# A stack of four graph networks on one core: sets by group, the entry to the second network and the output by node tile, angles on 128 rows

## The reference

```python
x = x + L0(h, ...)   # 7 graph convolutions with softmax over edges and a virtual node; a layer norm at the end
x = x + L1(h, ...)   # 4 blocks: conditioned layer norm, attention over edges, conditioned layer norm, dense pair
x = x + L2(h, ...)   # x @ wc + mean over edges of (x @ wn)[dst] + bias
x = x + L3(h, edge_attr, path_coeffs, src, dst, path_indices)
```

```python
x1 = x_nodes[src].reshape(-1, 16, 32)
x2 = x_edges.reshape(-1, 16, 32)
contrib = path_coeffs[None, :, None] * x1[:, i1, :] * x2[:, i2, :]     # 64 paths (i1, i2, i3)
edge_out = zeros.at[:, i3, :].add(contrib)
out = zeros.at[dst].add(edge_out.reshape(-1, 512))
```

## Time and profile before

| | us |
|---|---|
| median of 3 runs | 857.91 (856.36 to 860.02) |
| the profiled execution, own time | 857.5 |
| its span, first to last instruction | 855.7 |
| busy PE / DVE / ACT / POOL | 775.5 / 611.4 / 217.7 / 129.7 |
| mean granted TensorE clock | 0.968 of full |
| last network, from its first plain product | 541.3 to 855.7 |

### The profile page before, as it was taken

How to read it: one execution, slowest core, us unless ns; L and a number is a source line. 1 busy time by engine, 2 the same in 40 slices (tenths; PEclk the granted TensorE clock), 3 DMA queues, 4 the chain that set the end, 5 groups by cost and what they waited for, 6 DMA issues and landing times.

```text
span 855.7 us, 10601 instructions
## 1 busy us (share of the span) xinstructions
PE 775.5 (91%) x2972; PEld 501.2 (59%) x2972; DVE 611.4 (71%) x1581; ACT 217.7 (25%) x456; POOL 129.7 (15%) x145
## 2 busy tenths in 40 slices
PE   6888898898898999999999999889889997997998
PEld 2556455365365766667567554565676673683673
DVE  8876675675676534553553553799999999999895
ACT  6633123123121311311312212203304304304300
POOL 6000000000101000000000002611531451340000
PEclk9899999999999999999999999899989997997999
DMA  5813323214131423433342100742523443330000
GB/s 198 306 58 103 111 84 124 108 53 159 61 124 69 142 87 130 149 115 117 117 147 75 62 1 31 256 132 77 183 86 99 126 120 98 108 89 1 0 1 25
DMA packets 39175, 88.38 MB, mean 103 GB/s; under 512 B 3890, under 2 KB 4159, under 8 KB 39135
## 3 DMA queue, kind: packets, MB, share of 16 engines
q1 hardware_dynamic: 34496, 72.71, 25.2%
q0 software_dynamic: 4640, 15.21, 6.0%
HBM read 86.86 MB, written 1.05 MB: 103 GB/s over the span
## 4 chain that ended last, share of the span: by engine, by line
PE 51%; DVE 24%; issue 15%; DVEq 7%; ACT 1%; POOL 1%; DMA 0%; ACTq 0%; SPq 0%; POOLq 0%
PE PS L753 40%; DVE big L1504 8%; PE PS L1043 6%; DVE tail L1495 4%; DVEq L1470 3%; DVE tail L1514 2%; DVE prods L1514 2%; DVEq L1474 2%; DVE h L1128 1%; PE PS L909 1%; PE PS L762 1%; DVEq L1504 1%; DVEq L1514 1%; PE PS L858 1%; PE PS L954 1%
## 5 line engine op out<-in xcount | busy, mean ns | idle before, releaser
L753 PE MATMUL PS<-big 128*128 128x512 f32 (+1 forms) x368 | 137.2, 524 | 1.7 <-DVE big L1398 1.7
L1495 DVE SCALAR_TENSOR_TENSOR tail<-big,coef 128x448 f32 (+3 forms) x216 | 130.7, 616 | 3.1 <-issue 3.1
L1504 DVE TENSOR_TENSOR big<-big,tail 128x448 f32 (+3 forms) x216 | 120.9, 560 | 4.1 <-DVE tail L1495 3.1
L753 PEld LDWEIGHTS PS<-big 128*128 128x128 f32 x368 | 67.4, 190 | 63.6 <-issue 54.8
L753 PE MATMUL PS<-hT,big 128*128 128x256 f32 (+1 forms) x512 | 87.0, 329 | 4.4 <-ACT hT L678 4.4
L576 POOL DMA_INDIRECT big<-h_rows,src_i x58 | 77.2, 1331 | 85.6 <-PE PS L1043 62.9
L753 PEld LDWEIGHTS PS<-hT,big 128*128 128x128 f32 x512 | 77.5, 191 | 15.2 <-ACT hT L678 7.3
L550 POOL TENSOR_TENSOR rstd<-var,minus_half 128x1 f32<-128x1 f32 x36 | 21.6, 601 | 421.3 <-DVE var L1102 419.2
L1043 PE MATMUL PS<-big,hotd_more 128*128 128x512 f32 x176 | 76.5, 592 | 0.0
L1057 PE MATMUL PS<-hotd_more,tail 128*128 128x256 f32 x256 | 59.5, 387 | 0.0
L1043 PEld LDWEIGHTS PS<-big,hotd_more 128*128 128x128 f32 x176 | 33.4, 190 | 41.6 <-issue 41.6
...
## 6 DMA issues: line engine op xcount, KB each, us to landing
...
```

The costliest lines, as they stand in the source:

```text
L753: return pe.matmul(o, lhsT, rhs, start=start, stop=stop)
L1495: dve.scalar_tensor_tensor(out=prod[:, slot, tiles, :], in0=xs[:, tiles, bass.ds(i1, EXT)], scalar=coef[:, row:row + 1], in1=xe[:, tiles, ...
L1504: dve.tensor_tensor(o, o, prod[:, slot, tiles, :], ALU.add)._wait_ge(path_step, max(product_at[slot], added_at[0])).then_inc(path_step, 1)
```

## The change

- `SETS_OF` goes from 8, 6, 5, 5, 5 to 8, 7, 6, 6, 4, with new orders of the blocks for groups 1 to 4. The turns of the sets' sums in the last group stand between four sets instead of five.
- VectorE fills nothing of the sums any more: ScalarE fills tiles 0 to 6, GpSimd the rest, and VectorE waits for two parts instead of three. VectorE fills the PSUM half of set 3 with zeros, between the copies of picked rows, and set 3 starts on it without a start flag.
- The entry to L1: `first_norm` does all steps of node tile 0 and then all of node tile 1; GpSimd's roots follow that order; TensorE makes the first tables once the last convolution's statistics are there, and 3 fill products follow them instead of 6.
- L2: ScalarE takes each turned tile out in two halves of 256 columns, and TensorE waits for each half.
- The output: of the last six edge tiles TensorE adds all parts of node tile 0 first, then those of node tile 1 (`node_summed`), and VectorE's two last additions wait for their own node tile.
- The angles: `emb` is 128 rows x 128 columns (two times 64 rows), `fw1` is loaded twice, so SP issues seven loads for them instead of five; the two steps of rounding are one instruction; GpSimd sets up four strips of frequencies; TensorE makes two products of 128 columns with a wait between them.

The diff, cut to its core:

```diff
-ORDER = [[0, 1, 2, 3, 4, 5, 6, 7], [2, 0, 3, 1, 4, 5, 6, 7], [3, 0, 4, 1, 5, 6, 7, 2], [3, 0, 4, 1, 5, 6, 7, 2],
-         [3, 0, 4, 1, 5, 6, 7, 2]]
-SETS_OF = [8, 6, 5, 5, 5]
+ORDER = [[0, 1, 2, 3, 4, 5, 6, 7], [1, 2, 0, 3, 4, 5, 6, 7], [2, 0, 3, 1, 4, 5, 6, 7], [2, 0, 3, 1, 4, 5, 6, 7],
+         [4, 0, 5, 1, 6, 2, 7, 3]]
+SETS_OF = [8, 7, 6, 6, 4]
...
-ZERO_CUT = (2, 8)
+ZERO_CUT = 7
...
-FILL_L1_IN, FILL_L3 = (11, 6), 8
+FILL_L1_IN, FILL_L3 = (11, 3), 8
...
-        emb = region(7)[0:2 * NF, 0:N]
-        turns = region(7)[0:2 * NF, N:2 * N]
-        turn_part = region(7)[0:2 * NF, 2 * N:3 * N]
-        freq = sb("freq", [2 * NF, 4])
-        freq_i = sb("freq_i", [2 * NF, 1], I32)
-        fw1 = sb("fw1", [2 * NF, NC])
+        emb = region(7)[:, 0:P]
+        turns = region(7)[:, N:N + P]
+        turn_part = region(7)[:, 2 * N:2 * N + P]
+        freq = sb("freq", [P, 4])
+        freq_i = sb("freq_i", [P, 1], I32)
+        fw1 = sb("fw1", [P, NC])
...
-            sp.dma_start(emb, A["node_vec1"].rearrange("n a -> a n").to_broadcast([2 * NF, N])).then_inc(noise_in, 16)
-            sp.dma_start(fw1[:], A["L1_gnn_f_w1"]).then_inc(noise_in, 16)
+            for t in range(NT):
+                both = slice(t * 2 * NF, (t + 1) * 2 * NF)
+                sp.dma_start(emb[both, :], A["node_vec1"].rearrange("n a -> a n")[:, t * P:(t + 1) * P].to_broadcast([2 * NF, P])
+                             ).then_inc(noise_in, 16)
+                sp.dma_start(fw1[both, :], A["L1_gnn_f_w1"]).then_inc(noise_in, 16)
...
-            link(pool.tensor_scalar(turns, turns, ROUND, None, ALU.add))
-            link(pool.tensor_scalar(turns, turns, -ROUND, None, ALU.add))
+            link(pool.tensor_scalar(turns, turns, ROUND, -ROUND, ALU.add, ALU.add))
...
-            inverse_root(LN_L1_IN, var_in, rstd_in)
-            with pool.Fori(0, 2 * BLOCKS) as k:
+            for t in range(NT):
+                pool.wait_ge(ln_var, LN_L1_IN * 2 + (2 * t + 1))
+                pool.tensor_tensor(rstd_in[:, t:t + 1], var_in[:, t:t + 1], minus_half[:, t:t + 1], ALU.pow).then_inc(ln_est, 1)
+                pool.wait_ge(ln_var, LN_L1_IN * 2 + (2 * t + 2))
+                pool.tensor_tensor(rstd[:, t:t + 1], var[:, t:t + 1], minus_half[:, t:t + 1], ALU.pow).then_inc(ln_est, 1)
+            with pool.Fori(1, 2 * BLOCKS) as k:
...
-                pool.memset(part[SUM_AT[g]][:, ZERO_CUT[1]:SIZES[g], :], 0.0).then_inc(acc_zero, 1)
+                pool.memset(part[SUM_AT[g]][:, ZERO_CUT:SIZES[g], :], 0.0).then_inc(acc_zero, 1)
...
-                act.activation(hT[:, :, t * P:(t + 1) * P], turned_tile(t), ACT.Relu, bias=zero).then_inc(yT_ready, 1)
+                for some in (slice(0, 2), slice(2, CT)):
+                    act.activation(hT[:, some, t * P:(t + 1) * P], turned_tile(t)[:, some, :], ACT.Relu,
+                                   bias=zero).then_inc(yT_ready, 1)
...
-                cut = part[SUM_AT[g]][:, ZERO_CUT[0]:ZERO_CUT[1], :].rearrange("p j d -> p (j d)")
-                act.activation(cut, zero.to_broadcast([P, (ZERO_CUT[1] - ZERO_CUT[0]) * D]), ACT.Copy).then_inc(acc_zero, 1)
+                cut = part[SUM_AT[g]][:, 0:ZERO_CUT, :].rearrange("p j d -> p (j d)")
+                act.activation(cut, zero.to_broadcast([P, ZERO_CUT * D]), ACT.Copy).then_inc(acc_zero, 1)
...
-            mm(PS[0:NC, 6, 0:N], fw1[:], emb, True, True).then_inc(cond_a, 1)
+            for t in range(NT):
+                both = slice(t * 2 * NF, (t + 1) * 2 * NF)
+                if t:
+                    pe.wait_ge(cond_a, 1)
+                mm(PS[0:NC, 6, t * P:(t + 1) * P], fw1[both, :], emb[both, :], True, True).then_inc(cond_a, 1)
...
-            pe.wait_ge(st_set, LN_L1_IN * 2 + 2)
+            pe.wait_ge(st_set, LN_L0_LAST * 2 + 2)
...
-                pe.wait_ge(yT_ready, TURNED * BLOCKS + (t + 1))
                 for c in range(CT):
+                    if c % 2 == 0:
+                        pe.wait_ge(yT_ready, TURNED * BLOCKS + (2 * t + c // 2 + 1))
...
-                                    start=g == 0 and j == 0, stop=True, skip_group_check=True)
+                                    start=g == 0 and j == 0 and SETS - SETS_OF[g] + i != 3, stop=True,
+                                    skip_group_check=True)
...
-                        turn_sums((0, 2, 4, 5)[i - 1], (2, 4, 5, 6)[i - 1])
+                        turn_sums((0, 2, 4)[i - 1], (2, 4, 6)[i - 1])
...
-            sum_tiles(GROUPS - 1, SPLIT_TILE, SIZES[-1], STEP_AT[GROUPS])
+            pe.wait_ge(path_step, STEP_AT[GROUPS])
+            for t in range(NT):
+                for j in range(SPLIT_TILE, SIZES[-1]):
+                    ins = pe.matmul(PS[:, t, :], hotd(j)[:, t * P:(t + 1) * P], part[SUM_AT[-1]][:, j, :],
+                                    start=False, stop=True, skip_group_check=True)
+                ins.then_inc(node_summed, 1)
...
-            for t in range(NT):
+            def first_norm(t):
                 link(dve.scalar_tensor_tensor(out=xn[:, t, :], in0=h[:, t, :], scalar=mv[:, t, 0:1],
                                               in1=gb[:, 0, :], op0=ALU.subtract, op1=ALU.mult))
-            for t in range(NT):
                 dve.wait_ge(ln_est, LN_L0_LAST * 2 + (t + 1))
                 link(dve.scalar_tensor_tensor(out=x[:, t, :], in0=xn[:, t, :], scalar=rstd[:, t:t + 1],
                                               in1=x[:, t, :], op0=ALU.mult, op1=ALU.add))
                 stats(t, x).then_inc(st_set, 1)
-            for t in range(NT):
-                dve.wait_ge(st_set, LN_L1_IN * 2 + (t + 1))
+                dve.wait_ge(st_set, LN_L1_IN * 2 + (2 * t + 1))
                 link(dve.bn_aggr(mv[:, t, :], st[:, t, :]))
                 dve.tensor_scalar(var_in[:, t:t + 1], mv[:, t, 1:2], LN_EPS, None, ALU.add).then_inc(ln_var, 1)
                 link(dve.tensor_scalar(h[:, t, :], x[:, t, :], mv[:, t, 0:1], 0.0, ALU.subtract, ALU.max))
                 stats(t, h).then_inc(st_set, 1)
-            def first_var(t):
-                dve.wait_ge(st_set, LN_BLOCK * 2 + (t + 1))
+                dve.wait_ge(st_set, LN_L1_IN * 2 + (2 * t + 2))
                 link(dve.bn_aggr(mv[:, t, :], st[:, t, :]))
                 dve.scalar_tensor_tensor(out=var[:, t:t + 1], in0=var_in[:, t:t + 1], scalar=ln_eps,
                                          in1=mv[:, t, 1:2], op0=ALU.mult, op1=ALU.add).then_inc(ln_var, 1)
-            def cond_norm(k, t, variance=None):
-                if variance is None:
-                    aggregate(k + LN_BLOCK, t)
-                else:
-                    variance(t)
+                table_norm(0, t, LN_L1_IN * 2 + (2 * t + 2))
+            def table_norm(k, t, root):
                 dve.wait_ge(tab_done, k * 4 + (2 * t + 1))
                 link(dve.scalar_tensor_tensor(out=xn[:, t, :], in0=h[:, t, :], scalar=mv[:, t, 0:1],
                                               in1=PS[:, 4 + t, :], op0=ALU.subtract, op1=ALU.mult))
-                dve.wait_ge(ln_est, (k + LN_BLOCK) * 2 + (t + 1))
+                dve.wait_ge(ln_est, root)
                 dve.wait_ge(tab_done, k * 4 + (2 * t + 2))
                 dve.scalar_tensor_tensor(out=xn[:, t, :], in0=xn[:, t, :], scalar=rstd[:, t:t + 1],
                                          in1=PS[:, 6 + t, :], op0=ALU.mult, op1=ALU.add).then_inc(y_ready, 1)
+            def cond_norm(k, t):
+                aggregate(k + LN_BLOCK, t)
+                table_norm(k, t, (k + LN_BLOCK) * 2 + (t + 1))
...
-                cond_norm(0, t, first_var)
+                first_norm(t)
...
+                if j == 2:
+                    dve.wait_ge(picked_kept, 2)
+                    dve.memset(set_bank(3), 0.0).then_inc(picked_kept, 1)
+            dve.wait_ge(picked_kept, BY_PE + 1)
             for g in range(GROUPS):
...
-                    if at == 0:
-                        dve.memset(part[SUM_AT[g]][:, 0:ZERO_CUT[0], :], 0.0).then_inc(acc_zero, 1)
...
-                            dve.wait_ge(acc_zero, (g + 1) * 3)
+                            dve.wait_ge(acc_zero, (g + 1) * 2)
...
-                dve.wait_ge(tile_summed, ET)
+                dve.wait_ge(node_summed, t + 1)
```

28 lines of the change are left out of this document (14 added, 14 removed).

## The result

The changed kernel takes 844.88 us, the median of four runs (843.90 to 846.91). The kernel before, run beside it on the same chip, takes 858.26 (856.36 to 860.02, four runs). The ratio is 0.984, with a 95% interval of 0.982 to 0.987: faster by 13.4 us or 1.6%. The prediction was 844.7, between 840.5 and 850.5.

A forecast was written before the change was run, and what follows sets the result against it. VectorE was taken to set the pace in the last network from 541 on, until TensorE's work is longer. Terms -9.0 - 0.6 - 2.3 - 0.3 - 1.0 = -13.2 took 857.9 to 844.7, range 840.5 to 850.5.

The forecast's parts named there:

- Group 0: First group of the last network: eight sets before and after, one VectorE fill lost, -0.8.
- rival 5: Gap after VectorE's fill stays as a wait, costing up to 0.8 in group 0: 845.5; counted within the forecast's 0.62.
- Groups 1 to 3: Last network: VectorE needs 178.2 together, TensorE 180.1, so TensorE is longer by 1.9 and runs without a pause.
- wrong if VectorE waits for used sets in groups 1 to 3: Last network, sign against the forecast: the new orders were to fit, with margins of 0 to 0.8.
- Last group: Last network, four sets for five: VectorE waits 1.3 ahead of set 6; last tiles start at 821.6 instead of 830.63, -9.0.
- Last tiles and output: End of the last network: VectorE's first final addition no longer lies behind TensorE's end, -0.6; both engines level.
- Entry: Entry to the second network: tile 0 turned 3.3 earlier, tile 1 at 269.7 instead of 272.02, -2.3; worst bound 0.
- Third network: ScalarE hands the turned tile over in halves, 0.69 becoming about 0.35 ahead of the first matmul, tile 0 only: -0.3.
- Start: GpSimd's shorter angle chain gives VectorE's first comparison loop 1.6 back; taken as -1.0, between +0.3 and -2.5.
- Rival 3: At the start, the port VectorE and GpSimd share locks for whole instructions, giving 1.8 more: 842.9; chance 0.08.
- rival 1: Last network: TensorE's chain, without slack from group 1 to set 4 of the last group, slips: 847 to 850; chance 0.17.
- rival 4: Last network: TensorE's granted clock falls without a pause; 36 of the chain's 235 at the lower level make 862; chance 0.04.

## Why the prediction was right

It came out at 844.7 for 844.9, and of its terms most hold within 0.3. Step by step:

- **Group 0**: -0.8, measured -0.82. The gap behind the first plain products is 0.51 without the fill, and the whole 0.8 is gained all the same, so rival 5 falls.
- **Groups 1 to 3**: TensorE 59.5, 60.3, 60.3, measured 59.5, 60.4, 60.5, with no pause at clock 1.00. VectorE was to need 178.2 and needed 179.1 (its groups begin at 583.65, 642.22, 702.70 and 762.80). Of these 0.9, 0.5 are the 63.3 that I read for groups 2 and 3 where VectorE's own starts give 63.5, and 0.4 is the wait at 607.32, for the set that group 1 had a margin of 0 for. By the text's own sign ("wrong if VectorE waits for used sets in groups 1 to 3") this is a small failure of the order inside group 1. It cost nothing, as TensorE's 180.4 is longer.
- **Last group**: VectorE's wait ahead of set 6, forecast 1.3, is 1.0. The start of the last tiles was mis-sized by 0.8: from set 4 used to the end of the first half I had 25.0 and it took 25.1, and set 4 was free at 209.7 and not 209.3, with 0.35 more to VectorE's start. So group 0 and the last network bring 8.5 where I had 9.0 with a deduction for TensorE's restart. Its restart (810.88) was there, but ended level with VectorE.
- **Last tiles and output**: -0.6, measured -0.55. The two engines are level at the end as worked out.
- **Entry**: tile 0 3.3 earlier and tile 1 2.3, measured 3.29 and 2.32 against the end of the first network. What the text missed stands behind it: it said that TensorE has eleven microseconds of its own work there, and so nothing would be lost. VectorE is later with tile 1, and TensorE waits 0.21 for it at 284.80. In all 0.5 is lost over the second network, a term that the sum put at nothing; it comes back when the entry is undone.
- **Third network**: -0.3, measured -0.2.
- **Start**: -1.0, measured -1.38 at the first turn and -1.56 at VectorE's loop, where the text had 1.6. The mechanism is shown by moving the chain. Rival 3, the locked port, gives nothing more. But of the 1.38 only 1.19 are there at the end of the first network. The first network's length depends on where the lower clock falls, between 222.6 and 225.0 in kernels that do the same work there. I had not thought of that at all.
- **Slack**: rival 1 (TensorE's chain slips) and rival 4 (the clock falls in a fed stretch) did not come, in either trace of the changed kernel. No row from group 1 to set 5 shows less than 1.00.

The sum was too large by 1.0 on the profile's scale (13.2 for 12.2), and the median came out better than the profile (13.4). That both meet within 0.2 is partly luck. Two ingredients of it are known. The wait of 1.71 that the text counted among the gains was 0.32 in the execution of the kernel before with six matmuls more. And the 13.4 itself was 11.3 when both kernels were measured again; against that, 13.2 is too large by 1.9. The mechanism held, and the total hit closer than its terms did.
